# The first stage of a fused kernel: another order of its four batches, one bias product for four tiles

## What is computed

```python
x = x + _L0_xattn_ref(_layernorm(x, axis=-1), ctx_1024, w_sim, b_sim, W_qv, b_qv)

# encoder_hc: normalised x; decoder_hq: ctx_1024
Sim = (encoder_hc @ w1)[:, :, None] + (decoder_hq @ w2)[:, None, :] + jnp.einsum('bid,bjd->bij', encoder_hc * w3, decoder_hq) + b_sim[0]
A = jax.nn.softmax(Sim, axis=2)
hq_hat = jnp.einsum('bij,bjd->bid', A, decoder_hq)
Batt = jax.nn.softmax(jnp.max(Sim, axis=2), axis=1)
hc_bar = jnp.einsum('bi,bid->bd', Batt, encoder_hc)[:, None, :]
feats = jnp.concatenate([encoder_hc, hq_hat, encoder_hc * hq_hat, encoder_hc * hc_hat], axis=-1)
hcq = feats @ W_qv + b_qv
```

## Time and profile before

| | |
|---|---|
| median of 3 runs | 2084.4 us (2081.66 to 2086.53) |
| the profiled execution | 2087.44 us, its span 2085.6 us |
| busy over the span | PE 91%, DVE 69%, POOL 69%, ACT 67% |
| first stage | 0 to 109.7 us of the span |
| PE granted clock, mean | 0.96 of full |

### The profile page before, as it was taken

One profiled execution on the slowest core, in us unless ns is written; L12 is line 12 of the kernel. 1 busy time (PEld: TensorE's weight loads), 2 busy tenths in 40 slices (PEclk: granted clock), 3 DMA queues, 4 the chain that ended last, 5 costly groups with the idle time before them and its releaser, 6 DMA issues. The chain is left out here.

```text
span 2085.6 us, 77661 instructions
## 1 busy us (share of the span) xinstructions
PE 1895.0 (91%) x32069; PEld 1312.6 (63%) x32069; DVE 1446.0 (69%) x2609; ACT 1395.4 (67%) x2781; POOL 1445.9 (69%) x1837
## 2 busy tenths in 40 slices
PE   5648999999999999999999999999999999669958
PEld 4526666666666666666666666666666666456648
DVE  2357687778776877777777867787778786245546
ACT  1157777787777777777777777777787777235425
POOL 1158887888788878887788778877888787112334
PEclk9779999999999999999999999999999999769969
DMA  2011131111311113111113111121111111030002
GB/s 96 0 34 48 48 96 45 46 48 46 95 46 48 46 46 96 48 48 55 40 41 102 55 40 36 41 81 31 30 33 31 30 30 33 2 99 1 18 30 76
DMA packets 67088, 99.85 MB, mean 48 GB/s; under 512 B 15367, under 2 KB 51608, under 8 KB 65970
## 3 DMA queue, kind: packets, MB, share of 16 engines
q1 hardware_dynamic: 65234, 91.72, 15.3%
q0 software_dynamic: 1504, 3.17, 0.4%
HBM read 44.50 MB, written 21.45 MB: 32 GB/s over the span
## 5 line engine op out<-in xcount | busy, mean ns | idle before, releaser
L1074 PE MATMUL b_bank_proj<-layer_weights,b_stream_t 128*128 128x512 f32 x1152 | 589.4, 613 | 34.0 <-DVE b_plain_moved L948 17.9
L948 DVE TENSOR_TENSOR b_plain_moved<-b_bank_proj,b_rope 128x1024 f32<-128x1024 f32 x384 | 464.0, 1219 | 191.8 <-ACT b_squares L834 137.8
L759 POOL TENSOR_TENSOR b_rotated<-b_plain_moved 128x1024 f32<-128x1024 f32 x192 | 453.5, 2362 | 23.1 <-DVE b_plain_moved L948 18.7
L774 POOL TENSOR_TENSOR b_rotated<-b_rotated,b_inv_norm 128x1024 f32<-128x1024 f32 x192 | 365.2, 1902 | 15.6
L834 ACT ACTIVATE b_squares<-b_bank_proj 128x512 f32<-128x512 f32 x384 | 229.1, 597 | 116.1 <-PE b_bank_proj L1074 111.6
L865 ACT ACTIVATE b_k_t<-b_bank_shared 64x512 f32<-64x512 f32 x384 | 226.5, 590 | 119.9 <-PE b_bank_shared L1082 117.4
L1074 PEld LDWEIGHTS b_bank_proj<-layer_weights,b_stream_t 128*128 128x128 f32 x1152 | 186.9, 192 | 136.1 <-issue 45.7
L779 POOL TENSOR_TENSOR b_probs<-b_probs,b_inv_sum 128x512 f32<-128x512 f32 x192 | 200.3, 1044 | 90.1 <-DVE b_inv_sum L969 88.7
L856 ACT ACTIVATE b_q_t<-b_bank_shared 64x512 f32<-64x512 f32 x384 | 225.7, 588 | 34.3 <-PE b_bank_shared L1082 31.4
L1082 PE MATMUL b_bank_shared<-const_tables,b_rotated 128*128 128x128 f32 x1536 | 233.1, 277 | 15.6 <-POOL b_rotated L774 15.2
L1101 PEld LDWEIGHTS b_bank_scores<-b_k_t,b_q_t 128*32 128x32 f32 x12288 | 184.5, 111 | 98.9 <-issue 95.8
(11 more groups left out here) (320 smaller groups left out, 2866.8 us busy)
## 6 DMA issues: line engine op xcount, KB each, us to landing
b_v_shifted<-b_v SPq DMA_DIRECT2D x96, 384.0 KB, 3.5
sorted_rows<-constants SPq DMA_DIRECT2D x135, 129.0 KB, 3.4
layer_weights<-L_ffn_Wqkv SPq DMA_DIRECT2D x6, 1536.0 KB
b_v_shifted<-b_v SPq DMA_DIRECT2D x72, 128.0 KB, 3.4
layer_weights<-L_ffn_w SPq DMA_DIRECT2D x16, 256.0 KB, 5.2
layer_weights<-L_ffn_Wo SPq DMA_DIRECT2D x6, 512.0 KB
c_sorted_in<-sorted_rows SPq DMA_DIRECT2D x23, 129.0 KB, 2.1
layer_weights<-L_ffn_W SPq DMA_DIRECT2D x6, 341.0 KB
```

Source lines behind the costliest of these rows:

```text
L759: nc.gpsimd.tensor_tensor(out=turned[:, k, :], in0=pm[:, k, 0, :], in1=pm[:, k, 1, :], op=ALU.add).then_inc(add_done, 1)
L774: nc.gpsimd.tensor_tensor(out=tk, in0=tk, in1=repeat_last(rn[:, k, :], DH), op=ALU.mult).then_inc(rope_done, 1)
L948: nc.vector.tensor_tensor(to, src.to_broadcast(shape), tab.to_broadcast(shape), ALU.mult).then_inc(mul_done, 1)
L1074: nc.tensor.matmul(out, xs[:, b, t * P:(t + 1) * P], w, start=True, stop=True).then_inc(proj_full, 1)
```

## The change

On PE, `scores` now first writes the bias of all four tiles with one product of 308 columns (the row `urow` read four times) and accumulates the four tile products on it; `sums` has one product of ones with the new `bws` instead of four. `bws` is the sum of a partition's batch weights, which ACT's `weights` now gives by its accumulator. The negation of the global maximum leaves `shares` for a step `negative` of its own. POOL does `highest(0)`, `highest(1)`, `bias(0)`, `highest(2)`, `bias(1)`, `highest(3)`, `bias(2)`, `bias(3)`. DVE normalises all four batches ahead of the first `highest`. The orders of PE, ACT and DVE are written out anew.

```diff
--- before.py
+++ after.py
@@ -173,6 +173,7 @@
         hT = m.sb("hat_t", [P, B, SEQ])
         ehT = m.sb("normed_hat_t", [P, B, SEQ])
         bw = m.sb("batt", [P, B, TILES])
+        bws = m.sb("batt_own_sum", [P, B])
         rb = m.sb("inv_batt_sum", [P, B])
         hc = m.sb("hc_bar", [P, B])
         weff = m.sb("w_eff", [P, B, P])
@@ -240,8 +241,10 @@
 
                 for b in range(B):
                     first(b)
+                highest(0)
                 for b in range(B):
-                    highest(b)
+                    if b + 1 < B:
+                        highest(b + 1)
                     bias(b)
                 for b in range(B):
                     second(b)
@@ -265,7 +268,8 @@
 
                 def weights(b):
                     act.wait_ge(max_neg, b + 1)
-                    nc.scalar.activation(bw[:, b, :], nm[:, b, :], ACT.Exp, bias=nmx[:, b:b + 1], scale=-1.0).then_inc(batt, 1)
+                    nc.scalar.activation(bw[:, b, :], nm[:, b, :], ACT.Exp, bias=nmx[:, b:b + 1], scale=-1.0,
+                                         accum_out=bws[:, b:b + 1]).then_inc(batt, 1)
 
                 def probs_t(b):
                     act.wait_ge(pT_full, b + 1)
@@ -277,17 +281,26 @@
 
                 for b in range(B):
                     context(b)
-                for k in range(B + 3):
-                    if k < B:
-                        normed_t(k)
-                    if 2 <= k <= B + 1:
-                        weights(k - 2)
-                    if 1 <= k <= B:
-                        exponent(k - 1)
-                    if 2 <= k <= B + 1:
-                        probs_t(k - 2)
-                    if 3 <= k:
-                        hat_t(k - 3)
+                normed_t(0)
+                normed_t(1)
+                normed_t(2)
+                exponent(0)
+                normed_t(3)
+                exponent(1)
+                weights(0)
+                exponent(2)
+                probs_t(0)
+                weights(1)
+                exponent(3)
+                probs_t(1)
+                hat_t(0)
+                weights(2)
+                hat_t(1)
+                probs_t(2)
+                weights(3)
+                hat_t(2)
+                probs_t(3)
+                hat_t(3)
 
             @block.vector
             def _(dve):
@@ -326,10 +339,12 @@
                 def shares(b):
                     dve.wait_ge(s_exp, b + 1)
                     nc.vector.reciprocal(ri[:, b, :], sm[:, b, :]).then_inc(ri_done, 1)
+                    dve.wait_ge(ri_done, b + 1)
+                    nc.vector.tensor_tensor(prn[:, b, :, :], pr[:, b, :, :], repeat_last(ri[:, b, :], CTX), ALU.mult).then_inc(p_normed, 1)
+
+                def negative(b):
                     dve.wait_ge(max_all, b + 1)
                     nc.vector.tensor_scalar(nmx[:, b:b + 1], mxa[:, b:b + 1], -1.0, None, ALU.mult).then_inc(max_neg, 1)
-                    dve.wait_ge(ri_done, b + 1)
-                    nc.vector.tensor_tensor(prn[:, b, :, :], pr[:, b, :, :], repeat_last(ri[:, b, :], CTX), ALU.mult).then_inc(p_normed, 1)
 
                 def context_weights(b):
                     dve.wait_ge(b_full, b + 1)
@@ -374,30 +389,34 @@
                     keys(b)
                 statistics(2)
                 normalise(1)
-                highest(0)
                 statistics(3)
                 normalise(2)
+                normalise(3)
+                highest(0)
                 shares(0)
                 highest(1)
-                normalise(3)
-                context_weights(0)
+                negative(0)
                 shares(1)
                 highest(2)
+                negative(1)
+                shares(2)
+                context_weights(0)
+                highest(3)
+                negative(2)
+                shares(3)
                 product(0)
                 context_weights(1)
-                shares(2)
-                residual(0)
-                highest(3)
+                negative(3)
                 product(1)
                 context_weights(2)
-                shares(3)
+                residual(0)
+                product(2)
+                context_weights(3)
                 stream(0)
                 residual(1)
-                product(2)
-                context_weights(3)
+                product(3)
                 stream(1)
                 residual(2)
-                product(3)
                 stream(2)
                 residual(3)
                 stream(3)
@@ -421,10 +440,11 @@
                     pe.wait_ge(eT_done, b + 1)
                     pe.wait_ge(gT_done, b + 1)
                     pe.wait_ge(u_done, b + 1)
-                    for t in range(TILES):
-                        out = bk_n[b][:, t * CTX:(t + 1) * CTX]
-                        nc.tensor.matmul(out, eT[:, b, t * P:(t + 1) * P], gT[:, b, :], start=True, stop=False)
-                        last = nc.tensor.matmul(out, ones[0:1, :], urow[:, b, :], start=False, stop=True)
+                    nc.tensor.matmul(split(bk_n[b][:, 0:TILES * CTX], CTX), ones[0:1, :], repeat_mid(urow[:, b, :], TILES),
+                                     start=True, stop=False, skip_group_check=True)
+                    for t in range(TILES):
+                        last = nc.tensor.matmul(bk_n[b][:, t * CTX:(t + 1) * CTX], eT[:, b, t * P:(t + 1) * P], gT[:, b, :],
+                                                start=False, stop=True, skip_group_check=True)
                     last.then_inc(s_full, 1)
 
                 def sums(b):
@@ -433,8 +453,7 @@
                     pe.wait_ge(max_own, b + 1)
                     for t in range(TILES):
                         nc.tensor.matmul(bk_n[b][:, 0:1], e[:, b, t, :], bw[:, b, t:t + 1], start=(t == 0), stop=(t == TILES - 1))
-                    for t in range(TILES):
-                        last = nc.tensor.matmul(bk_n[b][:, 1:2], ones, bw[:, b, t:t + 1], start=(t == 0), stop=(t == TILES - 1))
+                    last = nc.tensor.matmul(bk_n[b][:, 1:2], ones, bws[:, b:b + 1], start=True, stop=True)
                     last.then_inc(b_full, 1)
 
                 def probs_t(b):
@@ -466,18 +485,30 @@
                 pe.wait_ge(w_in, 16 * NIN)
                 for b in range(B):
                     key_bias(b)
-                for k in range(B + 3):
-                    if k < B:
-                        normed_t(k)
-                    if 2 <= k <= B + 1:
-                        sums(k - 2)
-                        probs_t(k - 2)
-                    if 1 <= k <= B:
-                        scores(k - 1)
-                    if 2 <= k <= B + 1:
-                        hat(k - 2)
-                    if k >= 3:
-                        out(k - 3)
+                normed_t(0)
+                normed_t(1)
+                scores(0)
+                normed_t(2)
+                scores(1)
+                normed_t(3)
+                scores(2)
+                probs_t(0)
+                sums(0)
+                scores(3)
+                hat(0)
+                probs_t(1)
+                sums(1)
+                hat(1)
+                probs_t(2)
+                sums(2)
+                out(0)
+                hat(2)
+                probs_t(3)
+                sums(3)
+                out(1)
+                hat(3)
+                out(2)
+                out(3)
         m.clear_sems()
```

## The result

The changed kernel is faster: the ratio to the kernel before is 0.9922 (95% interval 0.9909 to 0.9936), medians 2067.85 and 2085.17 us of 15 runs each. That is about 16 us (13 to 19), where 26.6 were forecast, and 2067.85 lies above the range of 2052 to 2066. The profiled execution has a span of 2065.3 us.

A forecast was written before the change was run, and what follows sets the result against it. POOL's eight code loads, 52 us, were taken to bound the first stage; its end moving from 108.88 to 82.3 gives 26.6 us, so 2084.4 - 26.6 = 2057.8, given as 2058, range 2052 to 2066.

The forecast's parts named there:

- Loads as the clock: POOL, first stage: eight code loads, 52 us, set the pace; six remain, and two fewer give 13 us.
- h0: POOL's first reduce: forecast to start at 25.4, from POOL free at 19.6 plus a code load of 5.8.
- h1: POOL's second reduce: no code load ahead of it, but it waits for its maximum until 26.9.
- h3: POOL's fourth and last reduce: forecast to start near 56 and to be done at 56.4.
- The head and the scores: Start of the first stage: POOL free at 19.6, the 308-column product 1.1 us, first scores done at 21.5.
- The tail: Behind POOL's last bias: DVE and POOL alternate, three times 4.58 us from 68.5, ending at 82.3 if PE's clock rises.
- page's clock rule: A case given 0.05 within the forecast's 0.78; the prediction as given doesn't spell the rule out.
- Rival 1: POOL: a code load also stands ahead of the second reduce, 4.7 us later, 2062.5; chance 0.07.
- rival 2: PE stays at 1.2 GHz through the first stage's tail, which ends at 84.8; total 2060.3; chance 0.07.
- rival 3: The batches don't wait for the loads; only saved work counts, 11.6 us in all, 2072.8; chance 0.05.
- rival 4: Slower: the six remaining loads get longer, sharing DMA engines with next-stage weights; at twice their length 2096; chance 0.02.
- the wall: End of the first stage: all engines drain after DVE's last instruction at 108.88; the next stage starts at 109.72.

The follow-up runs named there:

- old_pool: The changed kernel with POOL's old order, reduce and bias in turn for each batch, PE's stream unchanged: 2080.78 us, ratio 0.9965 to the kernel before.
- before: The kernel before the change, unaltered, with which each other kernel was compared: median 2085.17 us.
- p96: The changed kernel plus 24 one-by-one products (96 instructions) behind PE's first output: 2057.84 us, ratio 0.9856 to the kernel before.
- after: The changed kernel, unaltered: median 2067.85 us, ratio 0.9922 to the kernel before.
- before_shifted: The kernel before with 160 no-operations at the start of PE's stream, which don't stand in PE's trace: ratio 1.0004.
- p128: The changed kernel plus 32 one-by-one products (128 instructions), 24 behind PE's first output and 8 behind the last: 2059.29 us, ratio 0.9865.
- p168: The changed kernel plus 42 one-by-one products (168 instructions), 24 behind PE's first output and 18 behind the last: ratio 0.9895.
- two_loads: p96 with all POOL reduces first and all biases after, two code changes instead of six: 2050.62 us, ratio 0.9827.
- before_p160: The kernel before plus 40 one-by-one products (160 instructions), twenty each behind the scores of the first two batches: ratio 1.0056.

## Why the prediction was right or wrong

**Loads as the clock: right.** The idle times ahead of the changes of code are 5.72 to 6.00 and 6.73 to 6.92 us, against 5.64 to 5.98 and 6.90 to 7.42. h0 started at 25.50 (25.4 forecast), h1 at 26.46 (26.9), h3 at 55.39 (56.0), the last bias ended at 65.08 (66.0). `old_pool` shows the two loads to be worth 12.3 us of the stage, by the forecast 13 less the 1 of the wait of h1. The Trainium skill (GPSIMD Engine Reference, Instruction dispatch) has 5.95 us for freshly loaded code; the trace agrees for the reduce and has 6.73 to 7.42 for the way back. (By the chain's own terms that price would end the last bias 3.2 us sooner, not 3.4.)

**The head and the scores: right.** POOL was free at 19.78 (19.6 forecast). One product of 308 columns took 1.32 us from its start to the next (1.1 forecast, 0.64 to 1.84 as bounds), and the first maximum began at 21.59 (21.5):

```profile
18.25 1.39 PE L443 MATMUL a_bank_n<-a_key_bias,const_tables 1*128 1x308 f32 x2
19.57 1.99 PE L446 MATMUL a_bank_n<-a_keys_t,a_normed_t 128*128 128x77 f32 x8
21.59 0.48 DVE L335 TENSOR_REDUCE a_neg_max<-a_bank_n 128x4 f32<-128x308 f32 x1 [0.67 <-PE a_bank_n L446]
```

**The tail: right.** PE's clock rose within it: outputs at 0.21 us an instruction until 66.99, at 0.11 from 68.27. That it rose in time is in part luck: in the first outputs it rose at about 50.8, was low again at 54.2, after PE had gone idle, and had risen again at 67.9. The chances also give 0.05 to a page's clock rule. No run here shows such a rule, and the changed kernel speaks against an early rise: PE worked without a break from 17.20 to 40.3 us, all of it at the low level.

```profile
66.56 0.63 PE L478 MATMUL a_bank_k<-a_w_qv,a_normed_hat_t 128*128 128x128 f32 x2
66.99 1.45 PE L468 MATMUL a_bank_n<-a_probs_t,a_ctx 77*128 77x512 f32 x2
68.27 0.39 PE L476 MATMUL a_bank_k<-a_w_eff,a_normed_t 128*128 128x128 f32 x2
68.50 0.39 PE L477 MATMUL a_bank_k<-a_w_qv,a_hat_t 128*128 128x128 f32 x2
```

DVE and POOL set the end, with 4.58 us for the last residual, its statistics and the stream, to the digit that of the earlier trace rows:

```profile
76.87 0.69 DVE L367 TENSOR_TENSOR residual<-a_bank_k,residual 128x512 f32<-128x512 f32 x1
...
80.34 1.11 DVE L381 TENSOR_SCALAR stream<-residual,a_mean_var,a_rstd 128x128 f32<-128x128 f32 x4 [1.46 <-POOL a_rstd L240]
```

The stage ended at 81.45, forecast 82.3. Rival 1 (a load ahead of h1) fell by the 0.59 us there, rival 2 by the clock, rival 3 by `old_pool`, and rival 4 by loads that got no longer. (The chances of a faster kernel add up to 0.97, not 0.96.)

**The step that failed** is this sentence of the prediction: "A microsecond won ahead of the wall should come off the whole." The wall holds for time, all engines do start anew behind it. It doesn't hold for the position in the stream. The change altered the second stage without touching it, by taking 96 instructions out ahead of it. No rival had this. I had costed the removed products by their time, hidden work that costs nothing, and not as a shift of everything behind them. In the trace of before it could have been seen: PE's waits for "issue" in the second stage, 7.6 us at L1130 alone, had no releaser, and I asked neither where they lie nor whether they would stay. The sum for the first stage was right: 26.6 us forecast, 27.4 measured. The term that was left out, the changed kernel against p96, is 10 to 12 us by the medians, 14 to 15 by the ratios. That p96's 2057.84 us meets the forecast 2058 is luck: the kernel before had 2087.86 in that comparison, not 2084.4, so p96 is 30.0 us below it, and its second stage is 4.8 us shorter than before's, which wasn't forecast.

**The mark that I named for it** ("a stage that ends 26 us sooner while the total doesn't follow, if the next stage meets a lower clock") was met in its first half. The clock isn't the cause by itself: p96 and `after` start the second stage in the same state and at the same time. But it takes part. All eight kernels at places 160 and 208 have four to eight drops of the clock in the second stage, the five others at places 0, 32 and 72 (before, before_shifted, p96, p128, p168) two to six, and two_loads, also at place 0, seven. Many drops come with the stops: 28 of the 75 in all 14 traces begin at a block-end stop or within 1.5 us behind its end, where such times make up 3% of the stretch; the four of the kernel before are none of these, and four of the six of the changed kernel are.

**What stays open.** The idle time at block ends differs by 7.8 us between before and after, and by 9.2 between before and before_p160, whose second stages differ by 6.8 and 15.0. The rest may be the drops of the clock that come with the stops, or the variation of a single execution; no run separates them. The Trainium skill (Runtime: NRT & Kernel Launch, Instruction fetch mechanics) says that each engine's instructions are refilled in 16 KiB blocks of 256 instructions over a DMA queue of its own, and that "The cost of crossing a 16 KiB boundary is one DMA tail-bump, mostly hidden." The trace agrees on the blocks, by 256 packets of 16 KB. On the cost it disagrees: 22 of 233 crossings stopped PE for 0.45 us or more, up to 1.72, in the changed kernel. Most crossings are hidden, as the page has it; of the 54 that fall in the products of probabilities with the values, the second of two dense loops in a row, 16 stopped. That PE waits there for the next block is read from the times of the packets, by their number; what passes in the 1.2 to 1.7 us between landing and resuming isn't shown.

## What to carry to other kernels

Where a long unrolled stage follows the one you edit, count the instructions that the edit adds to or takes from each engine's stream, and compare the later stages of the two traces, not the totals alone; if they differ, move the code by a few cheap instructions that do stand in the stream, and judge the edit by the best place of each kernel. On GpSimd, look first at what alternates between two kinds of code: the order decides how many loads of 6 to 7 us there are. As long as they are the clock, what is saved beside them costs nothing and gives nothing, and only what lies ahead of the first load or behind the last one shows. A written barrier separates the times of two stages, not their positions.

## What the runs showed of the hardware that I had not expected

- PE stops at the ends of blocks of 256 of its own instructions: 12 to 26 us in a second stage of 1709 to 1729 us, single stops without another engine up to 2.07 us. Of the changed kernel's 22 stops, 12 to 16 come back at the same instruction in each other trace with the same place. Whether a crossing costs anything depends on how fast PE passes the block before it: 171 of the 251 stops stand in one loop of 64 products of 32 columns that follows another such loop.
- PE never passed a block end earlier than 1.06 us after the landing of the packet that is due, and each stop ended 1.18 to 1.70 us after it.
- A no-operation on PE took no place in its stream: 96 and 160 of them left the records and the remainder of the stops as they were. One-by-one float32 products took four places each; 48 of their instructions' matmuls passed in 1.33 us.
- The changed kernel's 15 runs spread more than those of the kernel before: 2060.7 to 2080.8 us against 2079.8 to 2091.3. Whether the place does this isn't shown; p96's are four, between 2055.5 and 2059.7, and p128's five lie between 2053.3 and 2063.8.
